# A macaron block on one core: later attention groups' splits made in the convolution, rows in plane order, loads a group earlier

## The reference

```python
x = x + 0.5 * ffn(layernorm(x))
x = x + attn(layernorm(x))
x = x + 0.5 * ffn(layernorm(x))

def ffn(x):       # 8 experts, sign weights
    routing = softmax(x @ gate_w.T)                       # 2048 x 8
    return (x * (routing @ in_scale)) @ sign(w).T * (routing @ out_scale) + bias

def attn(x):      # convolution of 3 taps to 3*256 channels, then blocks of 128 tokens, 16 heads of 64
    q, k, v = split(conv3(x) + conv_b)
    qh, kh, vh = q @ wq + bq, k @ wk + bk, v @ wv + bv
    p = softmax(where(causal, qh @ kh.T / 8, -1e9))
    return ((p @ vh) @ wo + bo) @ proj_w + proj_b
```

## Time and profile before

| | |
|---|---|
| median of 3 runs | 1066.28 us (1061.52 to 1067.0) |
| profiled execution | 1063.77 us, span 1062.0 us |
| TensorE busy | 928.4 us (87%) |
| VectorE busy | 715.6 us (67%) |
| ScalarE busy | 453.2 us (43%) |
| GpSimd busy | 370.4 us (35%) |

### The profile page before, as it was taken

One profiled execution on the slowest core, in us unless ns is written; L12 is line 12 of the kernel. 1 busy time (PEld: TensorE's weight loads), 2 busy tenths in 40 slices (PEclk: granted clock), 3 DMA queues, 4 the chain that ended last, 5 costly groups with the idle time before them and its releaser, 6 DMA issues.

```text
span 1062.0 us, 15599 instructions
## 1 busy us (share of the span) xinstructions
PE 928.4 (87%) x4960; PEld 701.2 (66%) x4960; DVE 715.6 (67%) x1469; ACT 453.2 (43%) x1127; POOL 370.4 (35%) x307
## 2 busy tenths in 40 slices
PE   3898889886999899897987997899798888999997
PEld 2576667663334687686766886778577666688786
DVE  5677775567898888455487288368729946766652
ACT  3434444342134236144565356345625554334331
POOL 2145555564443210000121233214213441455555
PEclk8799999997999999998997999999999999999999
DMA  9333322321324341753002022211141264343233
GB/s 298 129 120 119 119 79 79 139 80 70 117 91 149 119 149 50 286 205 148 26 2 93 7 81 70 70 39 59 59 130 61 96 254 169 116 160 139 94 129 114
DMA packets 41469, 119.88 MB, mean 113 GB/s; under 512 B 5696, under 2 KB 14912, under 8 KB 40000
## 3 DMA queue, kind: packets, MB, share of 16 engines
q1 hardware_dynamic: 41408, 119.11, 32.3%
HBM read 87.64 MB, written 31.46 MB: 112 GB/s over the span
## 4 chain that ended last, share of the span: by engine, by line
PE 48%; DVE 15%; issue 5%; ACT 4%; DMA 2%; SPq 0%; POOL 0%; DVEq 0%; POOLq 0%; ACTq 0%
PE a_p_g L1762 16%; PE a_p_g L624 11%; PE c_p_m L1219 5%; PE c_p_m L1221 3%; PE c_p_m L1223 3%; PE c_p_m L1222 3%; PE a_p_s L1786 2%; ACT a_s L1559 2%; DVE a_sums L1663 2%; DVE a_s L1660 2%; PE a_p_o L1810 1%; DVE a_pt L1677 1%; DMA c_raw<-in_conv_w_dram 1%; DVE c_xs_lo L1625 1%; PE a_p_s L567 1%
## 5 line engine op out<-in xcount | busy, mean ns | idle before, releaser
L1492 POOL TENSOR_TENSOR a_s<-a_s,a_sums 128x512 f32<-128x512 f32 x64 | 66.6, 1040 | 309.1 <-DVE a_sums L1669 309.1
L276 POOL TENSOR_TENSOR f_y<-f_y,f_res 128x512 f32<-128x512 f32 x64 | 82.8, 1294 | 144.8 <-DVE f_y L478 144.5
L1559 ACT ACTIVATE a_s<-a_s,a_nmx 128x128 f32<-128x128 f32 x256 | 99.3, 390 | 44.5 <-DVE a_nmx L1665 44.5
L1762 PE MATMUL a_p_g<-c_xs_hi,x_room 128*128 128x512 f32 x256 | 97.7, 429 | 20.5 <-DVE c_xs_lo L1625 12.2
L624 PE MATMUL f_p_m<-f_wsign,f_a_hi 128*128 128x512 f32 x256 | 106.3, 415 | 0.0
L624 PE MATMUL f_p_m<-f_wsign,f_a_lo 128*128 128x512 f32 x256 | 102.6, 401 | 0.0
L624 PE MATMUL a_p_g<-f_wsign,f_a_hi 128*128 128x512 f32 x256 | 102.5, 400 | 0.0
L624 PE MATMUL a_p_g<-f_wsign,f_a_lo 128*128 128x512 f32 x256 | 100.4, 392 | 0.0
L1219 PE MATMUL c_p_m<-c_vf,c_ring_f 128*128 128x512 f32 x192 | 87.0, 610 | 9.3 <-DVE c_ring_f L896 6.2
L1221 PE MATMUL c_p_m<-c_vh,c_ring 128*128 128x512 f32 x192 | 76.3, 397 | 9.9 <-DVE c_ring L1102 8.1
L273 POOL TENSOR_TENSOR f_res<-f_res,f_hbias 128x512 f32<-128x512 f32 x64 | 83.2, 1300 | 0.0
(11 more groups left out here) (218 smaller groups left out, 2240.3 us busy)
## 6 DMA issues: line engine op xcount, KB each, us to landing
c_raw<-in_conv_w_dram SPq DMA_DIRECT2D x24, 768.0 KB, 4.3
f_w_raw<-in_w_t_dram SPq DMA_DIRECT2D x8, 1024.0 KB, 11.0
f_res<-in_x_dram SPq DMA_DIRECT2D x16, 512.0 KB, 4.0
x_after_ffn<-f_y SPq DMA_DIRECT2D x8, 1024.0 KB, 6.1
f_xin<-x_after_attention SPq DMA_DIRECT2D x8, 1024.0 KB, 7.2
f_res<-x_after_attention SPq DMA_DIRECT2D x16, 512.0 KB, 3.9
out_dram<-f_y SPq DMA_DIRECT2D x8, 1024.0 KB, 6.1
f_xin<-in_x_dram SPq DMA_DIRECT2D x7, 1024.0 KB, 8.2
```

The lines of the kernel that those rows point to most:

```text
L276: pool.tensor_tensor(y[:, p, t, h], y[:, p, t, h], res[:, t, h], ALU.add).then_inc(y_done, 1)
L1492: pool.tensor_tensor(s[:, r], s[:, r], sums[:, r].unsqueeze(2).broadcast_to([P, 4, P]), ALU.mult).then_inc(probs_ready, 1)
L1559: done = act.activation(s[:, r, h, :], s[:, r, h, :], ACT.Exp, bias=nmx[:, r, h:h + 1], scale=SCALE, accum_out=sums[:, r, h:h + 1])
L1762: mm = pe.matmul(p_g[:, bank, :], a, b, start=n == 0, stop=n == len(pairs) - 1)
```

## The change

- **Rows in plane order in FFN1 and at the output.** `src_planes` reads x so that partition 32 s + m of a tile holds token 4m+s. All x loads of FFN1 and its residual loads use it, one DMA for each tile; intermediate rows stay in that order in DRAM, and FFN2's stores put rows back with `dst_planes`, one DMA for each tile. `copy_normed` now reads and writes runs of 32. The causal mask is built in the same order, by four times three operations of GpSimd.
- **Loads one group earlier.** `load_x(g + 4)` stands in body g in place of `load_x(g + 3)`, after `t_full` of 4g+12, and group 3's load and statistics ahead of the loop, in FFN2 too. In a body the statistics move from the first quarter to the end of the last. `group_loop` is written out.
- **Splits of later groups in the third convolution stage.** For each chunk, ScalarE makes the high halves of tokens 512 to 2047 in four copies (`out_split_high`) and VectorE the low halves (`out_split_low`), and SyncE stores both as finished parts. Chunk 5's are made after the attention's first products.
- **Attention.** `load_y` and its splits are gone. GpSimd issues three 1 MB loads a group of finished parts (`load_xs`): v's at a group's beginning, q's and k's after its multiplies of rounds 11 and 12. The two wo products stand ahead of the next group's v products, and their results have a room of their own.

Its core (rooms, semaphores and counts left out):

```diff
 def group_loop(eng, body):
-    body(0, 0)
-    with eng.Fori(0, (NG - 4) // 2) as i:
-        body(2 * i + 1, 1)
-        body(2 * i + 2, 0)
-    for g in range(NG - 3, NG):
+    for g in range(NG):
         body(g, g % 2)
...
+    src_planes = src.rearrange("(g t m s) d -> g t s m d", t=FT, s=4, m=P // 4)
+    dst_planes = dst.rearrange("(g t m s) d -> g t s m d", t=FT, s=4, m=P // 4)
...
         def load_x(g, p):
-            if isinstance(g, int) and g == 2:
-                sp.wait_ge(t_full, 4)
-            sp.dma_start(xin[:, p], srcv[g]).then_inc(x_loaded[p], 16)
+            if isinstance(g, int) and g in (2, 3):
+                sp.wait_ge(t_full, 4 * g - 4)
+            if turn:
+                sp.dma_start(xin[:, p], srcv[g]).then_inc(x_loaded[p], 16)
+            else:
+                for t in range(FT):
+                    sp.dma_start(xin[:, p, t, :], src_planes[g, t]).then_inc(x_loaded[p], 16)
...
-            sp.dma_start(res[:, t, :], srcv[g][:, t, :]).then_inc(res_loaded[t], 16)
+            sp.dma_start(res[:, t, :], srcv[g][:, t, :] if turn else src_planes[g, t]).then_inc(res_loaded[t], 16)
...
-            if exists(g + 3):
-                sp.wait_ge(t_full, 4 * g + 8)
-                load_x(g + 3, 1 - p)
+            if exists(g + 4):
+                sp.wait_ge(t_full, 4 * g + 12)
+                load_x(g + 4, p)
...
             for q in range(4):
-                if q == 0 and exists(g + 3):
-                    stats(g + 3, 1 - p)
...
+                if q == 3 and exists(g + 4):
+                    stats(g + 4, p)
...
-            act.copy(Xp[:, k0:k0 + 4, :, quads].rearrange("p k s m -> p k m s"),
-                     bank[:].rearrange("p (k m s) -> p k m s", k=4, s=4)).then_inc(n_copied, 1)
+            act.copy(Xp[:, k0:k0 + 4, :, quads], bank[:].rearrange("p (k s m) -> p k s m", k=4, s=4)).then_inc(n_copied, 1)
...
+    def out_split_high(self, act, c, n):
+
+        if n == 0:
+            wait(act, self.high_stored, self.high_stores(c))
+            wait(act, self.out_low, c)
+            act.wait_ge(self.first_taken, 2 * NCH + c + 1)
+            act.wait_ge(self.y_final, c + 1)
...
+        act.copy(to, source).then_inc(self.out_high, 1)
+
+    def out_split_low(self, dve, c):
+
+        dve.wait_ge(self.out_high, 4 * c + 4)
+        if c < 2 * WC:
+            dve.tensor_tensor(self.Y_low[:, c, :, GTOK // 4:], self.Y[:, c, :, GTOK // 4:], self.room_high[:].bitcast(F32),
+                              ALU.subtract).then_inc(self.out_low, 1)
...
                     dve.tensor_tensor(low, whole, high.bitcast(F32), ALU.subtract).then_inc(w_lo, 1)
+                    conv.out_split_low(dve, m)
+            conv.out_split_low(dve, NCH - 2)
             for c in range(NCH - 1):
                 conv.first_split_low(dve, c)
...
-        after = [("v", 1, n) for n in range(2 * GT)] + after
+        after = after + [("v", 1, n) for n in range(2 * GT)]
...
+                if not last:
+                    pool.wait_ge(v_ready, 2 * GT * g + 2 * GT)
+                    load_xs(g + 1, 2)
...
+                    if not last and u in (11, 12):
+                        pool.wait_ge(gen_full, number(g, first, last, ("qk", 0, 4 * QUADS - 13 + u)) + 1)
+                        load_xs(g + 1, u - 11)
...
             for t in range(FT):
                 s2.load_res(0, t)
+            s2.load_x(3, 1)
             for t in range(GT):
                 store_x(AG - 1, t)
```

More of the change, by code:

```diff
@@ L851, in __init__, with planes @@
+        self.xs = [sb(f"xs{j}", [P, 2, WC, 4, GTOK // 4], F32R, at + XS_AT[j]) for j in range(3)]
         self.xs_hi, self.xs_lo = sem("xs_hi"), sem("xs_lo")
+        self.out_high, self.out_low = sem("out_high"), sem("out_low")
+        self.high_stored, self.low_stored = sem("high_stored"), sem("low_stored")
+    def planes(self, c, start, count):
+        planes = self.Y[:, c, :, start:start + count]
+        return planes if c < 2 * WC else planes.rearrange("p s (t m) -> p t s m", m=P // 4)
@@ new lines, in out_split_low @@
+    def out_split_low(self, dve, c):
+        dve.wait_ge(self.out_high, 4 * c + 4)
+        if c < 2 * WC:
+            dve.tensor_tensor(self.Y_low[:, c, :, GTOK // 4:], self.Y[:, c, :, GTOK // 4:], self.room_high[:].bitcast(F32),
+                              ALU.subtract).then_inc(self.out_low, 1)
+        else:
+            place = c - 2 * WC
+            dve.wait_ge(self.low_stored, 48 * (place + 1))
+            for n in range(4):
+                last = dve.tensor_tensor(by_position(self.Y_low[:, place, n, GTOK // 4:]), self.planes(c, GTOK // 4 + LATER * n, LATER),
+                                         by_position(self.room_high[:, n, :]).bitcast(F32), ALU.subtract)
+            last.then_inc(self.out_low, 1)
@@ L1565, in body @@
                             take(g, n + 1, flat(first, last).index(step) % 2, step)
-                    for c in range(NCH):
-                        if not last and u == SPLIT_ROUNDS[c]:
-                            reader = ("qk", 0, 4 * QUADS - 2 + c // 2) if c < 2 * WC else ("proj", -1, 2 * GT - 1)
-                            if reader in flat(first, last):
-                                act.wait_ge(gen_full, number(g, first, last, reader) + 1)
-                            split_high(g + 1, c)
                     if last and u >= UNITS:
@@ L1677, in body @@
                         dve.tensor_copy(pt[:, w % SLOTS].rearrange("p h t -> p (h t)"), p_t[:, w % 2, :]).then_inc(pt_copied, 1)
-                    for c in range(NCH):
-                        if not last and u == SPLIT_ROUNDS[c] + 1:
-                            split_low(g + 1, c)
                     if last:
@@ L1767, in body @@
                 steps = flat(first, last)
-                two_before = (BEFORE[-2:] if first else [("wo", -1, m) for m in range(WC)]) + steps
+                two_before = BEFORE[-2:] + steps
                 def general_product(step):
```

228 lines of the change are left out of this document (141 added, 87 removed).

## The result

The changed kernel takes 1136.15 us (median of 4 runs, 1133.74 to 1138.21) against 1066.64 before: a ratio of 1.0656, 95% interval 1.0608 to 1.0704. It is slower by 70 us, well above the range. The profiled execution has a span of 1133.5 us.

The account below looks back on a forecast made before the run. It took TensorE, busy 87% of the span, as the bound, so only its waits or late starts count. Terms 25 − 14 + 3 − 7 + 5 − 3 + 2 = +11 gave 1076 us; range 1044 to 1099.

Parts of the forecast that it names:

- Later bodies don't feel it: FFN1's later bodies: four engines need 23.2 us for x, residuals and store, within a 27 us body, so no loss.
- The start: Before body 0: group 3's rows land late on four engines, delaying TensorE; +25 us, bounds 0 and +36.
- the upper end: New 512 KB loads with outermost dimension 4: only four engines work on each, 5.2 us instead of 1.3.
- The rival of quicker engines: Four engines carry the loads at 35 KB per us each: start +8, total 1059 us; chance 0.12.
- The rival with sixteen engines: New loads spread over 16 engines: start 0, end −1, sum −17, total 1047 us; chance 0.20.
- Bodies: FFN1: contiguous copy into X and statistics moved to a body's last quarter; −14 us, bounds −8 and −20.
- Third convolution stage and its end: Added splits covered by free time, but the stage's end delays TensorE's restart; +3 us, 0 to +6.
- Ends of groups 0 to 2: Attention: split waits go, a load wait appears ahead of round 14; −7 us, bounds −12 and +4.
- Last group: Attention: with v last, residuals land later and the first projection's take comes 13.5 us in; +5 us, 0 to +8.
- The end: Last body's store: 512 KB on four engines takes 5.2 us against 2.6 for 1 MB on 16; +2 us.
- The late-load rival: Ends of attention groups: GpSimd-issued loads take 10 to 13 us instead of 5 to 7; +24, total 1100; chance 0.12.
- The late third stage: Rival, third convolution stage: VectorE's rings come 2 us late in five chunks; +10, total 1086 us; chance 0.08.

Follow-up runs that it names:

- experiment 2: Changed kernel, transfers still on four engines, with residual loads and store ahead of x's load on SyncE: 1119.22 us, 1.0534 of the kernel before.
- experiment 4: Kernel before, with only FFN1's x and residuals read by the plane pattern (outermost 4): 1100.79 us, ratio 1.0345.
- experiment 1: Changed kernel with each 512 KB four-plane transfer issued as four of 32 rows: 1065.32 us, 1.0022 of the kernel before.
- experiment 3: Changed kernel with transfers as four of 32 rows and residuals and store ahead of x's load: 1065.59 us, 1.0018 of the kernel before.
- experiment 5: experiment 1 with the next group's v products ahead of the wo products again: 1043.65 us, 0.9801 of the kernel before.
- experiment 9: Experiment 6 with GpSimd's first two bias additions ahead of its wait for v, v last: 1048.77 us, 0.9865 of the kernel before.
- Experiment 6: experiment 1, v last, with the last two residual loads ahead of the second network's loads in the last group: 1057.05 us, 0.9918 of the kernel before.
- experiment 7: experiment 1, v last, with q's and k's part loads issued one round earlier: 1052.99 us, 0.9881 of the kernel before.
- experiment 10: experiment 1 with v ahead of wo and q's and k's part loads one round earlier: 1032.19 us, 0.9708 of the kernel before.

## Why the prediction was wrong

**The step that failed** is "Later bodies don't feel it", for which it gave a body of 27 us and a need of 10.3 us for x, 10.3 for residuals and 2.6 for the store, 23.2 in all. So the loss in the bodies stood at nothing in the sum. The need is right and the conclusion is not. It took the queue as a throughput, as if its work were spread over the body. But the change moved x's load behind a wait that ends with a body's last transposes, and SyncE is in order: residuals and store, whose own waits had long ended, were issued behind it. From 98.54 us x's load is issued, from 99.69 the residuals, at 103.29 the store. Queued one after another on four engines they need until some 122 us by the 23.2 above, and VectorE, which waits for the store, goes on at 125.49. The rest of the body, some 11 us, follows. Three such bodies cost 11.0, 9.6 and 8.7 us, 29.3 in all. Experiments 2 and 4 show the two halves: with residuals first, or with the earlier wait, four engines do no harm to bodies; experiments 1 and 3 show that with sixteen engines the order does none either. The later wait stood in the change's own list, but the prediction didn't ask when each load is issued. Its sign did come: it had said that a body above 30 us would mean that residuals pace it.

**The start** had the right mechanism and too small a size: +25 forecast, +33.3 in the changed kernel and +33.0 in experiment 4, by group 0's first addition. The queue delivered group 3 at 77.3 us and not 72.3, and the 3 us that TensorE was to give back did not come. Why it was 5 us later stays open. SyncE's standing doesn't explain it by itself: the share was 0.24 or more in each stretch of 3 to 5 us from 5 us to group 3's landing, so the engines had work while SyncE stood. Of the signs, the share of 0.25 at 15 to 60 us did not come as said: over that stretch it was 0.58 at 166 GB/s, since the weights land in it.

**Sixteen or four.** The choice of the upper end was right, though not for the reason taken from the rows. The loads of the scales ran at a share of 1.10, all engines busy; their 191 GB/s say nothing of few engines, so as far as the rows go the choice was luck. The Trainium skill's rule (page "DMA: Bandwidth & Descriptors", section "Why a DMA increments its semaphore by 16 and not by 1"), by which the outermost dimension sets the number of engines, agrees with the runs: a share of 0.29 at 106 GB/s where that dimension is 4, and, from 5 to 8 us, 0.24 against 0.99 with 32. Which engines they are no run here shows. The rival of quicker engines falls: 106 GB/s over four are 26.5 KB per us each, not 35. The rival with sixteen engines was priced at −17. Experiment 1 measured what that case gives: 0, within half a per cent. So the terms for the rest were off as well, by some 16 us in the attention (+14.1 against before for the three stretches between groups, for −2) and by some 8 in the first network.

**Bodies** of FFN1: −14 forecast. In experiment 1 the first convolution product is 6.3 us early although group 0's first addition is 4.6 us late, which makes −10.8 between those marks: the bodies did get shorter, by three quarters of the forecast. The copy into X fell as said (606 ns for 1085). How much each of the two edits gave was not tried.

**Third convolution stage and its end**: +3 forecast, −0.8 measured in the changed kernel and −2.5 in experiment 1, over the whole convolution and the start of the attention. The added splits cost nothing that shows.

**Ends of groups 0 to 2**: a wait for the load ahead of round 14 was right in kind (1.7, 3.6 and 3.2 us in the three groups, forecast as some 4), and so were the lost split waits. What the −7 lacked is the start of the next group. The prediction said that "wo ahead of v costs nothing: its operands have their own room". It looked at operands and not at GpSimd, where the load of v's parts waits for v and two additions stand behind it. With v last these fall on the first scores: 5 to 6 us for groups 1 and 2, shown by experiments 5 and 9.

**Last group**: +5 forecast, +10.2 measured for the stretch. The take at 863.13 came 18.3 us after SyncE's first load of 844.81, which marks the group's start, and not 13.5, since the two additions also wait for two residual loads issued at 852.64, behind 7.8 us of other issues. Experiment 6, with the residuals first, gives 11 us back.

**Second network**: −3 forecast and −3.2 measured; VectorE's wait of 4.7 us for the load of the earlier trace rows is gone. **The end**: +2 forecast, +6.1 measured. The last body stores two tiles of 512 KB, 5.2 us each on four engines, and they queue: the share stays at 0.25 to 0.26, at 102 to 106 GB/s, from 1118 to 1131 us. With pieces of 32 rows the end is 5.2 us, for 5.8 before.

The late-load rival was wrong in price: GpSimd's loads land in 5.7 us. The late third stage did not occur.

## What to carry to other kernels

Look at the outermost dimension of every new transfer before its bytes: a 512 KB transfer over four planes ran at a quarter of the rate, and four pieces of 32 rows kept all engines busy again, if not at the full rate. A queue that has room on average can still be late: write down when each transfer is issued, because a wait moved on an in-order engine moves everything behind it, and then a body's transfers come in one burst. And when a product is moved, ask who waits for it on every engine, and what stands behind that wait. Here the change as a whole was worth 31 us against the kernel before, once its loads were in pieces, v stood first again and the parts came a round earlier.

## What the runs showed of the hardware

- While DMAs of 512 KB with an outermost dimension of 4 were alone in the queue, the share was 0.26 to 0.27 at 97 to 108 GB/s (stretches of 5 us from 45 to 75 us of the changed kernel). Behind such transfers the issue of a 32 KB load took up to 9.85 us on SyncE, and up to 1.87 us before.
- VectorE's operation on 128x4 numbers took 4.16 us in place of 0.17 while GpSimd added 128x1024 numbers twice, in 4.70 us, and 0.17 us where the additions stood elsewhere. In the kernel before, one that began at 794.24 us, in the second of the two additions of the earlier trace rows, took 2.32 us.
- Removing TensorE's waits for loads gave more than the waits: 12.6 us for 10.2 (experiment 7) and 13.1 for 9.5 (experiment 10 against 5, by the stretches). Over the three groups the mean granted clock rose with it, from 0.93 to 0.96 and from 0.96 to 0.99, and TensorE's busy time fell by 5.0 and 6.5 us. So the clock is likely the rest; it was not tried by itself.
